# One chunk of the shared expert issued one tile earlier, the first tile's factors read from PSUM, and residual parts moved

## The chip, the core and the metric

The kernel runs on one core of a Trainium2 chip. The metric is the device time of one execution, in microseconds. Matrix products run on TensorE (PE), elementwise work on VectorE (DVE) and ScalarE (ACT), small powers and indirect DMAs on GpSimd (POOL), and SyncE (SP) issues the plain DMAs. The engines run beside each other and meet only at semaphores, each in the order in which its code is written.

## The reference

The input x has 2 batches of 1024 tokens with 512 values, all float32. From a 2 x 512 conditioning vector c come six modulation rows per batch. In short:

```
sa, ca, ga, sb, cb, gb = silu(c) @ wmod            # ga, gb: |.| at least 0.25, sign kept
h = layernorm(x) * (1 + ca) + sa
x = x + ga * attn(h)     # own layernorm, Q, K, V; A = sum over tokens of cos(K) * cos(V) after a rotary;
                         # Y = (0.5 * A + 0.5) * Q @ W_out + b_out + h
h = layernorm(x) * (1 + cb) + sb
x = x + gb * ffn(h)      # 8 experts with 2 per token, H = 352, and a shared one with HS = 704:
                         # silu(h @ w_gate) * (h @ w_up) @ w_down
```

## The kernel before

**Tiles.** The 2048 tokens are 16 tiles of 128 rows. Four tiles are one group `g` of 512 tokens. Nearly every product is split in high and low parts: an operand is written as `hi` (rounded) by ACT and as `lo` (the rest) by DVE, and `product3` (L1805 to L1807) issues hi*hi, hi*lo and lo*hi. So a matrix that TensorE is to read is ready when DVE has written its lo part, and the semaphore for it is counted by DVE.

**Start.** DVE computes the modulated and normalised row of tile 0: `modulated(0)` subtracts the mean and multiplies by `bc_c` (L1139), multiplies by 1/std and adds `bc_s` (L1142), and takes statistics of the row (L1143). `bc_c` is one plus a row that TensorE spread into PSUM, copied by DVE (L1252). POOL computes the power -0.5, ACT writes the normalised row (L735), TensorE transposes it (L1853), and ACT and DVE write hi and lo (`tokens_hi`, `tokens_lo`, L1150). The K and V products of tile 0 end with a bias product (L1871), whose row is finished by `bias_rows` on DVE (L1162).

**K and V for all 16 tiles**, and then a stage that builds the combined matrices `mw` (`m_block`, `m_first`, `m_second`). From here the residual of a tile is prepared by `residual_part(t)` (L1330) on DVE, which reads the row that ACT normalised in `x_normed(t)`.

**Second rows.** For each tile t, TensorE computes the attention output (`y_matmul(t)`: 12 products and a bias product, L2172). It waits for `x2_ready >= t - 1`, that is for `second_rows(t - 2)` on DVE, which empties the bank. DVE adds the residual (`second_rows`, L1342), takes statistics, then runs `residual_part(t + 1)`, `tokens2_lo(t - 2)` (L1361) and, when POOL has the power, `ffn_rows(t)` (L1354, L1356), the input of the expert part. TensorE transposes the ffn rows of tile t - 2 (`transposes2`, L2180), ACT writes their hi part and DVE their lo part. For t < 4 DVE also makes the lo part of a quarter of the shared weights (L1106). At tile 6, DVE multiplies and splits the four late blocks of `mw` for the second batch (L1294, L1299), which `y_matmul(8)` waits for.

Five chunks of the shared expert's gate and up products (24 products of 512 columns each, operands `xt` and `sgu`) of group 0 lie between these tiles or behind them. The table `Y_CHUNKS` says behind which tile a chunk stands: chunk 0 behind tile 6, then 7, 10, 13. Chunk 0 waits for `t2_lo >= 4`, the lo parts of tiles 0 to 3, and chunk 1 for `s_mul >= 1`, DVE's product of chunk 0 (L1369). ACT applies silu behind the chunk (`s_silu_of`); hi and lo parts of the result (`s_hi_of`, `s_lo_of`) follow one tile later.

**Shared and routed experts.** The shared expert goes on for groups 1 to 3, then the down products. Between the last ones TensorE transposes the 5 sub-tiles gathered for the first expert (`turn_rows`, L2092; the places are `TURN_AT`). Step s >= 2 waits for the lo part of step s - 2 (`picked_lo`, L1670). DVE also finishes output rows here (`shared_rows`, L1475 and L1477), two instructions for each tile. Then the routed experts run in a loop and at the end.

Of the kernel before, what the change touches and what calls it, by code (L numbers as in the profile page):

```python
# [21 lines left out]
ALU, ACT, AX = mybir.AluOpType, mybir.ActivationFunctionType, mybir.AxisListType  # L22
# [39 lines left out]

FIRST = 3
M_BLOCKS = 2 * DC - 1
Y_CHUNKS = {6: 0, 7: 1, 10: 2, 13: 3}


MISC = ["sin_a", "cos_a", "s1", "c1", "sin_b", "cos_b", "q0", "q1", "q2", "q3", "mod", "qrow", "qbias", "a0", "a1"]
# [5 lines left out]
def build(nc, X, W_in, b_in, W_out, b_out, gamma, beta, gate_w, w_gate, w_up, w_down,  # L74
# [10 lines left out]
    with ctx:  # L85
# [620 lines left out]
        def _(act):  # L706
# [192 lines left out]
            def s_hi_of(g, m):  # L899
                n = NS * g + m  # L900
                r = SM[m]
                act.wait_ge(s_mul, n + 1)
                if n == 0:
                    act.wait_ge(y_mm, NB)
                if g:
                    act.wait_ge(s_down_mm, GT * g)
                nc.scalar.activation(gtS[0:r, m, 0, :], gbuf_of(n)[0:r, :], ACT.Copy).then_inc(s_hi, 1)
# [22 lines left out]
            for t in range(NT):  # L930
                if t >= 6 and t % GT == 2:
                    read_parts((t - 6) // GT)
                if t >= 2:
                    tokens2_hi(t - 2)
                if t + 2 < NT:
                    x_normed(t + 2)
                if t in (FIRST + 1, FIRST + 2):
                    m_block_out(2 * (t - FIRST - 1))
                    m_block_out(2 * (t - FIRST - 1) + 1)
                if t == NB - 2:  # L940
                    for i in range(DC):
                        m_block_hi_late(i)
                if t - 1 in Y_CHUNKS:
                    s_hi_of(0, Y_CHUNKS[t - 1])
                if t in Y_CHUNKS:
                    s_silu_of(0, Y_CHUNKS[t])

# [146 lines left out]
        def _(dve):  # L1094
            steps = [0]

            def link(ins):

                steps[0] += 1
                ins.then_inc(dve_step, 1)  # L1100
                dve.wait_ge(dve_step, steps[0])
# [27 lines left out]
            def modulated(t):  # L1129

                b, row = t // NB, hz[:, t % 2, :]
                dve.wait_ge(rs1_ready, t + 1)
                if t >= 2:
                    dve.wait_ge(z_ready, t - 1)
                if t == 0:
                    dve.wait_ge(s0_ready, 1)
                if t == NB:
                    dve.wait_ge(misc_read, MISC.index("c1") + 1)
                dve.scalar_tensor_tensor(row, xring[:, t % GT, :], mv1[:, t, 0:1], bc_c[:, b, :], ALU.subtract, ALU.mult)\  # L1139
                    .then_inc(x_read, 1)  # L1140
                dve.wait_ge(x_read, t + 1)
                link(dve.scalar_tensor_tensor(row, row, rs[:, 0, t:t + 1], bc_s[:, b, :], ALU.mult, ALU.add))  # L1142
                link(dve.bn_stats(st6[:, :], row))  # L1143
                link(dve.bn_aggr(mv2[:, t, :], st6[:, :]))
                dve.tensor_scalar_add(ve[:, 1, t:t + 1], mv2[:, t, 1:2], EPS)
                dve.tensor_scalar_mul(mv2[:, t, 0:1], mv2[:, t, 0:1], -1.0).then_inc(ve2_ready, 1)

            def tokens_lo(t):
                dve.wait_ge(t_hi, t + 1)
                dve.tensor_tensor(tokens(t, 1), chunked(bank[T_BANKS[t % 2]][:, :]), tokens(t, 0).bitcast(F32),  # L1150
                                  ALU.subtract).then_inc(t_lo, 1)
# [96 lines left out]
            dve.tensor_copy(b_col[:, 2:4], bank[COL_BANK][:, at + 2 * DC:at + 2 * DC + 2]).then_inc(gb_ready, 1)  # L1248
            dve.wait_ge(gb_ready, 1)
            x_statistics(1)  # L1250
            dve.wait_ge(spread_mm, 3)
            link(dve.tensor_scalar_add(bc_c[:, 0, :], bank[V_BANKS[0]][:, :], 1.0))  # L1252
            modulated(0)
            weights_lo(0)
            x_statistics(2)
            tokens_lo(0)
            bias_rows(0)
            modulated(1)
            weights_lo(1)
            bias_rows(1)  # L1260
            tokens_lo(1)
# [127 lines left out]
            m_block(0, 1)  # L1389
            read_misc("a1")  # L1390
            m_block_lo(0, 1)
            m_block(0, 2)
            scaled_q_lo(1, 0)
            m_block_lo(0, 2)
            m_block(0, 3)
# [2 lines left out]
            scaled_q_lo(1, 1)  # L1398
            y_bias_rows()
            scaled_q_lo(1, 2)  # L1400
            residual_part(0)
            scaled_q_lo(1, 3)
            dve.wait_ge(cb_in, 16)
            dve.wait_ge(sb_in, 16)
            for t in range(NT):
                second_rows(t)
                if t + 1 < NT:
                    residual_part(t + 1)
                if t >= 2:
                    tokens2_lo(t - 2)  # L1410
                if t == NB - 2:
                    for i in range(DC):
                        m_block_late(i)
                if t - 1 in Y_CHUNKS:
                    s_lo_of(0, Y_CHUNKS[t - 1])
                ffn_rows(t)
                if t == NB - 2:
                    for i in range(DC):
                        m_block_lo_late(i)
                if t < DC:  # L1420
                    shared_in_lo(t)
                if t in Y_CHUNKS:
                    s_mul_of(0, Y_CHUNKS[t])
# [339 lines left out]
            expert_lo(0, 0, 2)  # L1763
            for s in range(CT):
                picked_lo(0, 0, (s,))
                if s < 2:
                    shared_rows(3, (s,))
            shared_rows(3, (2, 3))
            turn_columns(0, 0)
            dve.wait_ge(loops_ready, 1)  # L1770
# [512 lines left out]
```

## Time and profile before

| | |
|---|---|
| median of 3 runs | 666.33 us (665.25 to 667.1) |
| the profiled execution | 664.12 us, span 662.3 us |
| PE busy | 641.1 us, 97% |
| DVE busy | 494.9 us, 75% |
| ACT busy | 268.8 us, 41% |
| mean granted TensorE clock | 0.993 of full |

The span is what lies between the first and the last record, and 1.8 us of the execution lie around it. A busy PE means that a product was in flight. What matters for a change that moves instructions is where TensorE stood idle, for whom it waited, and when the clock that the chip granted was lower. In rows of the timeline the first number is the start and the second the time from start to end; products overlap, so the next one starts 0.23 us after the last although each takes 0.39 us.

### The profile page before, as it was taken

What the parts mean: (1) busy time and instruction counts of PE and PEld (TensorE: products, weight loads), DVE (VectorE), ACT (ScalarE), POOL (GpSimd) and SP (SyncE); (2) the same over time, 40 slices, a digit from 0 to 9 for tenths busy, and PEclk for the clock granted to TensorE, in tenths of its full rate; (3) what the DMA queues carried; (4) which work ended last, traced back from release to release, by engine and by line L of the source; (5) the groups of instructions that cost most, each with busy time, mean ns of one, the idle gap of its engine ahead of it and who ended that gap; (6) DMA issues with size and microseconds to landing.
All of it is one profiled execution on the core that took longest, in us unless ns stands there. A gap on an engine that the chain in (4) does not pass through costs nothing.

```text
span 662.3 us, 10575 instructions
## 1 busy us (share of the span) xinstructions
PE 641.1 (97%) x3666; PEld 531.5 (80%) x3666; DVE 494.9 (75%) x1086; ACT 268.8 (41%) x525; POOL 164.8 (25%) x211
## 2 busy tenths in 40 slices
PE   7899999999998999999999999999999999999995
PEld 3577677777876787888888788798989899899994
DVE  3987779847899788647886684659769697786953
ACT  3555354443453443412102301445537455474530
POOL 1233233320111111100000002223644455443123
PEclk9999999999998999999999999999999999999998
DMA  8923031006234262513042052446877667666144
GB/s 331 395 58 108 34 96 33 32 17 207 79 113 142 96 208 103 159 54 106 0 133 82 17 163 83 121 139 192 173 141 214 80 196 162 150 183 106 49 61 63
DMA packets 41151, 80.80 MB, mean 122 GB/s; under 512 B 5019, under 2 KB 13229, under 8 KB 40566
## 3 DMA queue, kind: packets, MB, share of 16 engines
q1 hardware_dynamic: 33382, 62.06, 28.6%
q0 software_dynamic: 7728, 18.22, 15.0%
q8 instruction: 23, 0.38, 0.2%
q14 instruction: 18, 0.15, 0.1%
HBM read 58.88 MB, written 22.56 MB: 123 GB/s over the span
## 4 chain that ended last, share of the span: by engine, by line
PE 83%; DVE 11%; issue 2%; ACT 1%; POOL 1%; DMA 1%; SPq 0%; POOLq 0%; DVEq 0%
PE bank L1805 22%; PE bank L1807 22%; PE bank L1806 22%; PE bank L2117 5%; PE bank L2092 2%; PE bank L1935 1%; PE bank L2122 1%; PE bank L1871 1%; PE bank L1853 1%; DMA xring<-in_L_attn_X 1%; PE bank L2072 1%; PE bank L2180 1%; DVE st L1121 1%; POOL out_rows L679 1%; DVE hx L1354 1%
## 5 line engine op out<-in xcount | busy, mean ns | idle before, releaser
L1805 PE MATMUL bank<-ht,ew 128*128 128x256 f32 (+1 forms) x256 | 74.3, 290 | 0.0
L1805 PE MATMUL bank<-xt,sgu 128*128 128x512 f32 x176 | 70.1, 398 | 3.6 <-DVE xt L1361 2.0
L679 POOL DMA_INDIRECT out_rows<-y,si x35 | 54.8, 1565 | 75.4 <-DVE y L1734 66.0
L1806 PE MATMUL bank<-ht,ew 128*128 128x256 f32 (+1 forms) x256 | 73.1, 285 | 0.0
L1807 PE MATMUL bank<-ht,ew 128*128 128x256 f32 (+1 forms) x256 | 73.0, 285 | 0.0
L1807 PE MATMUL bank<-xt,sgu 128*128 128x512 f32 x176 | 69.3, 394 | 0.0
L1806 PE MATMUL bank<-xt,sgu 128*128 128x512 f32 x176 | 69.2, 393 | 0.0
L1805 PE MATMUL bank<-wkv,xt 128*128 128x512 f32 x128 | 53.8, 421 | 0.7 <-DVE xt L1150 0.7
L1806 PE MATMUL bank<-wkv,xt 128*128 128x512 f32 x128 | 50.5, 394 | 0.0
L1807 PE MATMUL bank<-wkv,xt 128*128 128x512 f32 x128 | 50.4, 394 | 0.0
L1806 PEld LDWEIGHTS bank<-ht,ew 128*128 128x128 f32 x256 | 48.3, 188 | 0.0
L1805 PEld LDWEIGHTS bank<-ht,ew 128*128 128x128 f32 x256 | 48.2, 188 | 0.0
L1807 PEld LDWEIGHTS bank<-ht,ew 128*128 128x128 f32 x256 | 48.2, 188 | 0.0
L659 POOL COPY gi<-gidx 128x5 int32 (+1 forms) x8 | 4.7, 583 | 170.3 <-DVEq L1643 130.6
L667 POOL DMA_INDIRECT picked<-h_d,gi x36 | 41.3, 1146 | 17.5 <-issue 8.5
L1805 PEld LDWEIGHTS bank<-xt,sgu 128*128 128x128 f32 x176 | 33.4, 190 | 10.9 <-DVE xt L1361 2.2
L610 POOL TENSOR_TENSOR rs<-ve,nhalf 128x1 f32<-128x1 f32 x16 | 15.4, 961 | 96.5 <-DVE ve L1123 96.5
L1807 PEld LDWEIGHTS bank<-xt,sgu 128*128 128x128 f32 x176 | 33.4, 190 | 7.2
L1806 PEld LDWEIGHTS bank<-xt,sgu 128*128 128x128 f32 x176 | 33.5, 190 | 6.4
L1805 PE MATMUL bank<-ew,gtR 128*128 128x512 f32 (+1 forms) x96 | 38.4, 400 | 0.0
L1807 PE MATMUL bank<-ew,gtR 128*128 128x512 f32 (+1 forms) x96 | 37.9, 395 | 0.0
L1806 PE MATMUL bank<-ew,gtR 128*128 128x512 f32 (+1 forms) x96 | 37.9, 394 | 0.0
(374 smaller groups left out, 1631.5 us busy)
## 6 DMA issues: line engine op xcount, KB each, us to landing
xring<-in_L_attn_X SPq DMA_DIRECT2D x32, 256.0 KB, 2.7
ewst<-in_L_ffn_w_gate SPq DMA_DIRECT2D x8, 704.0 KB
ewst<-in_L_ffn_w_up SPq DMA_DIRECT2D x8, 704.0 KB
slots<-in_L_wmod SPq DMA_DIRECT2D x4, 1024.0 KB, 7.0
x_d<-rows SPq DMA_DIRECT2D x16, 256.0 KB, 2.0
h_d<-hx SPq DMA_DIRECT2D x16, 256.0 KB, 2.0
xrow<-x_d SPq DMA_DIRECT2D x16, 256.0 KB, 2.7
out_rows<-xrow SPq DMA_DIRECT2D x16, 256.0 KB, 2.0
```

The source lines that it names most:

```text
L610: pool.tensor_tensor(rs[:, 2, t:t + 1], ve[:, 2, t:t + 1], nhalf[:, 0:1], ALU.pow).then_inc(rs3_ready, 1)
L667: pool.indirect_dma_start(out=picked[par][:, j, :], out_offset=None, in_=h2_d, in_offset=bass.IndirectOffsetOnAxis(ap=gi[:, par, j:j + 1], ...
L679: pool.indirect_dma_start(out=out, out_offset=bass.IndirectOffsetOnAxis(ap=si[0:CR[j], par, j:j + 1], axis=0), in_=y[0:CR[j], j, :], in_of ...
L1121: link(dve.bn_stats(st6[:, :], row))
L1354: link(dve.scalar_tensor_tensor(hx_of(t), rows_of(t), mv2[:, t, 0:1], bc_cb[:, b, :], ALU.subtract, ALU.mult))
L1805: nc.tensor.matmul(dst, a[0], b[0], start=first, stop=False)
L1806: nc.tensor.matmul(dst, a[0], b[1], start=False, stop=False)
L1807: return nc.tensor.matmul(dst, a[1], b[0], start=False, stop=last)
L1853: last = nc.tensor.transpose(bank[T_BANKS[t % 2]][:, k * P:(k + 1) * P], hz[:, 2 + t % 2, k * P:(k + 1) * P], ident[:, :])
L1871: nc.tensor.matmul(to, pairs4[:, :].to_broadcast([P, P]), (bk, bv)[i][:, :], start=False, stop=True)\
L2092: last = nc.tensor.transpose(bank[RT_BANKS[(par + s) % 2]][:, i * P:(i + 1) * P], picked[par][:, j, k * P:(k + 1) * P], ident[:, :])
L2117: nc.tensor.matmul(bank[to[c % 2]][0:n, 0:width], packed[:, k, i * P:i * P + n], tok[part][:, k, :], start=k == 0 and not part, stop=k == ...
```

## The change

It has four parts, and none changes what is computed.

- Tile 0's row is made in another way. `modulated_first` computes (x - mean) / std first, multiplies by one plus the row in PSUM, and adds `bc_s`. The copy `bc_c` follows behind it. `modulated(1)` moves ahead of `bias_rows(0)`.
- `residual_part(0)` and `residual_part(1)` move from the end of the matrix stage, and from tile 0 of the second rows, into the matrix stage.
- Chunk 0 of the shared expert stands behind tile 5 in place of tile 6 on TensorE, ACT and DVE. `tokens2_lo(3)` stands ahead of `residual_part(6)` on DVE. The hi and lo parts of the chunk stay at tile 7, by the new table `Y_PARTS`.
- `shared_rows` of tiles 12 and 13 stand behind steps 1 and 2 of the first expert's lo parts, in place of steps 0 and 1.

```diff
-Y_CHUNKS = {6: 0, 7: 1, 10: 2, 13: 3}
+Y_CHUNKS = {5: 0, 7: 1, 10: 2, 13: 3}
+Y_PARTS = {7: 0, 8: 1, 11: 2, 14: 3}
...
-                if t - 1 in Y_CHUNKS:
-                    s_hi_of(0, Y_CHUNKS[t - 1])
+                if t in Y_PARTS:
+                    s_hi_of(0, Y_PARTS[t])
...
+            def modulated_first():
+
+                row = hz[:, 0, :]
+                dve.wait_ge(rs1_ready, 1)
+                dve.tensor_scalar(row, xring[:, 0, :], mv1[:, 0, 0:1], rs[:, 0, 0:1], ALU.subtract, ALU.mult).then_inc(x_read, 1)
+                dve.wait_ge(spread_mm, 3)
+                dve.wait_ge(x_read, 1)
+                link(dve.scalar_tensor_tensor(row, bank[V_BANKS[0]][:, :], 1.0, row, ALU.add, ALU.mult))
+                dve.wait_ge(s0_ready, 1)
+                link(dve.tensor_tensor(row, row, bc_s[:, 0, :], ALU.add))
+                statistics_of_h(0)
...
-            dve.wait_ge(spread_mm, 3)
+            modulated_first()
             link(dve.tensor_scalar_add(bc_c[:, 0, :], bank[V_BANKS[0]][:, :], 1.0))
-            modulated(0)
             weights_lo(0)
             x_statistics(2)
             tokens_lo(0)
+            modulated(1)
             bias_rows(0)
-            modulated(1)
             weights_lo(1)
...
             m_block_lo(0, 1)
+            residual_part(0)
             m_block(0, 2)
+            residual_part(1)
             scaled_q_lo(1, 0)
...
                 second_rows(t)
-                if t + 1 < NT:
+                if t == GT + 1:
+                    tokens2_lo(t - 2)
+                if t and t + 1 < NT:
                     residual_part(t + 1)
-                if t >= 2:
+                if t >= 2 and t != GT + 1:
                     tokens2_lo(t - 2)
...
                 picked_lo(0, 0, (s,))
-                if s < 2:
-                    shared_rows(3, (s,))
+                if s in (1, 2):
+                    shared_rows(3, (s - 1,))
```

On DVE at the start, `hz` is the row of tile 0 (then of tile 1), `bk` the bias row and `wkv` the lo parts of the K weights. Before:

```order
L1252 TENSOR_SCALAR bc_c<-bank 128x512
L1139 SCALAR_TENSOR_TENSOR hz<-xring,mv,bc_c 128x512
L1142 SCALAR_TENSOR_TENSOR hz<-hz,rs,bc_s 128x512
L1143 BN_STATS st<-hz 128x6
L1144 BN_AGGR mv<-st 128x2
L1145 TENSOR_SCALAR ve<-mv 128x1
L1146 TENSOR_SCALAR mv<-mv 128x1
L1156 SCALAR_TENSOR_TENSOR wkv<-slots,gb_col,wkv 128x512 x4
```

The same place now:

```order
L1148 TENSOR_SCALAR hz<-xring,mv,rs 128x512
L1151 SCALAR_TENSOR_TENSOR hz<-bank,hz 128x512
L1153 TENSOR_TENSOR hz<-hz,bc_s 128x512
L1158 BN_STATS st<-hz 128x6
L1159 BN_AGGR mv<-st 128x2
L1160 TENSOR_SCALAR ve<-mv 128x1
L1161 TENSOR_SCALAR mv<-mv 128x1
L1267 TENSOR_SCALAR bc_c<-bank 128x512
L1171 SCALAR_TENSOR_TENSOR wkv<-slots,gb_col,wkv 128x512 x4
```

The row has three instructions of its own, and the copy `bc_c` moved from ahead of it to behind it.

On TensorE, ahead of chunk 0 of the shared expert (`xt,sgu`); `bh,pair` ends an attention product, `tmp,gw` are the gate's logits of group 0, `ident,hx` transposes of ffn rows. Before:

```order
L2172 MATMUL bank<-bh,pair 128x512
L2193 MATMUL bank<-tmp,gw 32x128 x16
L2180 MATMUL bank<-ident,hx 128x128 x4
L1805 MATMUL bank<-xt,sgu 128x512
L1806 MATMUL bank<-xt,sgu 128x512
```

Now:

```order
L1824 MATMUL bank<-mw,xt 128x512
L2189 MATMUL bank<-bh,pair 128x512
L2197 MATMUL bank<-ident,hx 128x128 x4
L1822 MATMUL bank<-xt,sgu 128x512
L1823 MATMUL bank<-xt,sgu 128x512
```

These are the attention product of tile 5 and the transposes of tile 3. The product of tile 6, the logits and the transposes of tile 4 now come behind the chunk.

On DVE at tile 5 (`xt` is the lo part of tile 3, `u` the residual of tile 6, `ewst` the product of chunk 0). Before:

```order
L1342 SCALAR_TENSOR_TENSOR rows<-u,mv,bank 128x512
L1121 BN_STATS st<-rows 128x6
L1122 BN_AGGR mv<-st 128x2
L1123 TENSOR_SCALAR ve<-mv 128x1
L1330 SCALAR_TENSOR_TENSOR u<-bc_c,std,xring 128x512
L1361 TENSOR_TENSOR xt<-bank,xt 128x4x128
L1354 SCALAR_TENSOR_TENSOR hx<-rows,mv,bc_gb 128x512
L1356 SCALAR_TENSOR_TENSOR hx<-hx,rs,bc_s 128x512
```

Now:

```order
L1356 SCALAR_TENSOR_TENSOR rows<-u,mv,bank 128x512
L1122 BN_STATS st<-rows 128x6
L1123 BN_AGGR mv<-st 128x2
L1124 TENSOR_SCALAR ve<-mv 128x1
L1375 TENSOR_TENSOR xt<-bank,xt 128x4x128
L1344 SCALAR_TENSOR_TENSOR u<-bc_c,std,xring 128x512
L1368 SCALAR_TENSOR_TENSOR hx<-rows,mv,bc_gb 128x512
L1370 SCALAR_TENSOR_TENSOR hx<-hx,rs,bc_s 128x512
L1383 TENSOR_TENSOR ewst<-ewst,bank 128x512
```

The lo part moved one instruction ahead, and the product of chunk 0 came in from the end of tile 6.

## Rows read from the trace of the kernel before

**Rows 1.** The page: busy us, share of the span and instructions of each engine.

```profile
PE 641.1 (97%) x3666; PEld 531.5 (80%) x3666; DVE 494.9 (75%) x1086; ACT 268.8 (41%) x525; POOL 164.8 (25%) x211
```

**Rows 2.** Waits of TensorE: line, releaser, us in total, times, longest.

```profile
PE bank L1805 <- DVE rows L1342: 2.3, 2, 1.2
PE bank L1853 <- ACT hz L735: 2.1, 2, 1.8
PE bank L1805 <- DVE xt L1361: 2.0, 1, 2.0
```

**Rows 3.** Stretches: length, busy us of five engines (instructions), granted clock, DMA.

```profile
207.00:208.00 1.00, 1.00 (x4) 0.81 (x3) 0.93 (x4) 0.00 (x0) 0.00 (x0) 0.50 0.96 356
```

**Rows 4.** Timeline of TensorE: start, us, line, operation, tiles, shapes, idle before.

```profile
196.12 0.60 PE L2180 MATMUL bank<-ident,hx 128*128 128x128 f32 x4
197.91 0.50 PE L1805 MATMUL bank<-mw,xt 128*128 128x512 f32 x1 [1.19 <-DVE rows L1342]
...
202.15 0.65 PE L2180 MATMUL bank<-ident,hx 128*128 128x128 f32 x4
...
204.81 0.50 PE L1805 MATMUL bank<-xt,sgu 128*128 128x512 f32 x1 [2.00 <-DVE xt L1361]
...
212.00 0.40 PE L1805 MATMUL bank<-mw,xt 128*128 128x512 f32 x1
...
215.14 0.60 PE L2180 MATMUL bank<-ident,hx 128*128 128x128 f32 x4
216.17 0.50 PE L1805 MATMUL bank<-xt,sgu 128*128 128x512 f32 x1 [0.43 <-DVE ewst L1369]
...
221.75 0.40 PE L1805 MATMUL bank<-mw,xt 128*128 128x512 f32 x1
```

**Rows 5.** Timeline of VectorE, tiles 2 to 6 of the second rows.

```profile
187.49 0.69 DVE L1361 TENSOR_TENSOR xt<-bank,xt 128x512 fp32r<-128x512 f32 x1
...
203.41 0.74 DVE L1330 SCALAR_TENSOR_TENSOR u<-bc_c,std,xring 128x512 f32<-128x512 f32 x1
204.07 0.69 DVE L1361 TENSOR_TENSOR xt<-bank,xt 128x512 fp32r<-128x512 f32 x1
...
206.11 0.75 DVE L1342 SCALAR_TENSOR_TENSOR rows<-u,mv,bank 128x512 f32<-128x512 f32 x1
...
215.43 0.68 DVE L1369 TENSOR_TENSOR ewst<-ewst,bank 128x512 f32<-128x512 f32 x1
```

**Rows 6.** Timeline of ScalarE, hi part of tile 0's ffn rows.

```profile
186.86 0.60 ACT L880 ACTIVATE xt<-bank 128x512 fp32r<-128x512 f32 x1
```

**Rows 7.** Timeline of VectorE, the start.

```profile
14.22 0.75 DVE L1139 SCALAR_TENSOR_TENSOR hz<-xring,mv,bc_c 128x512 f32<-128x512 f32 x1 [0.91 <-ACT bc_s L806]
...
15.80 0.69 DVE L1143 BATCH_NORM_STATS2 st<-hz 128x6 f32<-128x512 f32 x1
...
20.55 0.69 DVE L1150 TENSOR_TENSOR xt<-bank,xt 128x512 fp32r<-128x512 f32 x1
21.16 0.74 DVE L1162 SCALAR_TENSOR_TENSOR bk<-bk,nodd,bank 128x512 fp32r<-128x512 f32 x1
21.81 0.75 DVE L1139 SCALAR_TENSOR_TENSOR hz<-xring,mv,bc_c 128x512 f32<-128x512 f32 x1
...
24.46 2.73 DVE L1156 SCALAR_TENSOR_TENSOR wkv<-slots,gb_col,wkv 128x512 fp32r<-128x512 f32 x4
```

**Rows 8.** Timeline of TensorE, tile 0's bias product and tile 1's transposes.

```profile
23.96 0.19 PEld L1871 LDWEIGHTS bank<-bk,pairs 128*128 128x128 f32 x1
...
26.81 0.66 PE L1853 MATMUL bank<-ident,hz 128*128 128x128 f32 x4 [0.26 <-ACT hz L735]
```

**Rows 9.** Timeline of ScalarE, VectorE and TensorE at the first expert's transposes.

```profile
424.50 0.60 ACT L985 ACTIVATE ht<-bank 128x512 fp32r<-128x512 f32 x1 [2.37 <-PE bank L2092]
...
426.29 0.68 DVE L1670 TENSOR_TENSOR ht<-bank,ht 128x512 fp32r<-128x512 f32 x1
...
427.03 0.66 PE L2092 MATMUL bank<-ident,picked 128*128 128x128 f32 x4 [1.21 <-DVE ht L1670]
```

More of the change, by code:

```diff
@@ L1134, in modulated @@
                     dve.wait_ge(z_ready, t - 1)
-                if t == 0:
-                    dve.wait_ge(s0_ready, 1)
                 if t == NB:
@@ L1142, in modulated, with statistics_of_h @@
                 link(dve.scalar_tensor_tensor(row, row, rs[:, 0, t:t + 1], bc_s[:, b, :], ALU.mult, ALU.add))
-                link(dve.bn_stats(st6[:, :], row))
+                statistics_of_h(t)
+            def modulated_first():
[8 more added lines that the diff above has]
+                statistics_of_h(0)
+            def statistics_of_h(t):
+                link(dve.bn_stats(st6[:, :], hz[:, t % 2, :]))
                 link(dve.bn_aggr(mv2[:, t, :], st6[:, :]))
@@ L1400, in _ @@
             scaled_q_lo(1, 2)
-            residual_part(0)
             scaled_q_lo(1, 3)
@@ L1413, in _ @@
                         m_block_late(i)
-                if t - 1 in Y_CHUNKS:
-                    s_lo_of(0, Y_CHUNKS[t - 1])
+                if t in Y_PARTS:
+                    s_lo_of(0, Y_PARTS[t])
                 ffn_rows(t)
```

## The prediction

> **What bounds the kernel now.** The page comes first. TensorE is busy for 641.1 of 662.3 us [rows 1], so time is won or lost only where it stands idle or runs slowly. The waits of TensorE say where: 2.3 us in two waits for DVE's second rows, 2.1 us for ACT's normalised rows at the start, 2.0 us once for the lo part of a tile [rows 2]. The timeline of TensorE then places them. Around tiles 5 to 7 there are three waits, of 1.19, 2.00 and 0.43 us [rows 4], and the stretches show that the granted clock fell to half, 1.2 GHz, shortly after the second of them, and was there at 207 to 208 us [rows 3]. The reader is to see that chunk 0 of the shared expert took 204.81 to 212.00, 7.19 us, and chunk 1, the same 24 products at 2.4 GHz, 216.17 to 221.75, 5.58 us [rows 4]: the low clock cost 1.6 us. What bounds this stretch is DVE. It runs from tile 2 on without a stop worth naming, and it makes the lo parts that TensorE waits for [rows 5]. At the end of the shared expert TensorE waits 1.21 us more for DVE [rows 9]. So three places count, and I take them one by one.
>
> **The chunk behind tile 5.** TensorE has done the transposes of tile 3 at about 196.5 (they start at 196.12 [rows 4]). Now the product of tile 6 came next, and it waited 1.19 us. In the changed kernel the chunk comes next, and it needs the lo part of tile 3. DVE wrote that from 204.07 to 204.76 [rows 5]. Put ahead of the residual part, which runs from 203.41 to 204.07, it starts at 203.41 and ends at 204.10, 0.66 us earlier. TensorE starts the chunk 0.05 us behind, at 204.15, and not at 204.81. So of the 7.6 us from 196.5 to 204.15 it does nothing, where before 4.7 us of useful work, tile 6's product, logits and transposes, stood among them.
>
> Could DVE be earlier? The two residual parts that leave this chain are worth 0.66 us each. The one of tile 1 lay beside POOL's power at tile 0, so its going saves nothing. The one of tile 0 lets DVE run 0.66 us ahead, but only up to the lo part of tile 0. That starts at 187.49, right behind ACT's hi part (186.86 + 0.60 = 187.46 [rows 5, 6]), which waits for TensorE's transposes. TensorE works there without a wait, so this point doesn't move and DVE waits off what it had won. In the matrix stage the two residual parts fall into idle time of DVE ahead of `m_block(0, 2)` and of `scaled_q_lo(1, 0)`, where it waits for TensorE and ACT: nothing. Had that cover not been there, they would cost at most 2 x 0.66 on DVE, and TensorE has work to do meanwhile.
>
> From 204.15 on the pieces have the lengths that the timeline shows [rows 4]. The chunk takes 5.58. Tile 6's product, logits and transposes took 197.91 to the end of the transposes, 202.15 + 0.65 = 202.80, less 0.24 because the next product may start that much ahead of a modelled end: 4.65, and 0.1 less again since the product doesn't start from a stop. Tile 7's product with logits and transposes takes from 212.00 to 215.14 + 0.60 less 0.24: 3.5. Chunk 1 takes 5.58. The sum is 223.4 for the start of tile 8's product, which stood at 221.75 [rows 4]: later by 1.6 us, with no low clock in it, where the 221.75 has 1.6 us of it. The small wait of 0.43 for chunk 0's product is gone, for DVE now makes that product while TensorE runs tile 6.
>
> What is late next? DVE can't take tile 6's rows before TensorE has made its product, at 204.15 + 5.58 + about 3.2 = 212.9 in place of 206.11. From there to the end of the four late lo parts of `mw` it took 206.11 to 215.43, 9.3 us [rows 5], and some 0.2 more as the lo part of tile 4 now waits for its transposes. So 222.5, against 223.4 when TensorE asks for them. 0.9 us is left. DVE then has about 3 us of arrears on tiles 7 and 8, which TensorE doesn't feel: it asks for tile 7's rows at tile 9.
>
> **The clock.** Before, waits of 1.19 and 2.00 us close together were followed by the low clock, 1.2 GHz [rows 3, 4]. The changed kernel has one wait of over 7 us in that place. The nearest row is that fall, with its cost of 1.6 us, and I take it again. The ends are 0 (no fall, or one that has passed within the wait) and 5.6 us (the whole chunk at half speed costs its 5.58 us once more). So the stretch costs 1.6 + 1.6 = 3.2 us, between 1.6 and 7.2.
>
> The Trainium skill (TensorE: Matmul & The Clock Gate, the section on why this matters for your kernel) says that a long gap between bursts of matmuls brings the clock back to the lower level and that only sustained work raises it again. The trace agrees for a wait of 2.00 us. By this rule, too, it is worse to gather several short waits into one long one, and the fall would be sure: the 3.2 us stand. Without the rule the sum would be the same, with more weight on its lower end.
>
> **The start.** The three instructions of tile 0's row: the first is done while the copy `bc_c` ran, the second ends about when ACT's `bc_s` comes (14.22 is when DVE went on behind it [rows 7]), and the third, an add of 0.69 us as others of 512 columns [rows 7], puts the statistics at 14.94 in place of 15.80: 0.86 us earlier. But behind them comes the copy, which I size like the add, 0.69 and 0.03 for its hand-over, ahead of the lo parts of the weights. So `tokens_lo(0)` starts at 20.55 - 0.86 + 0.72 = 20.41, and TensorE's K products only 0.14 us earlier. The first instruction, a form that no row of the trace shows with 512 columns out of SBUF, may take anything up to the 0.75 of its neighbours without mattering.
>
> Then `modulated(1)` stands ahead of `bias_rows(0)`. It starts at 20.41 + 0.61 = 21.02 and takes 2.65 (21.81 to 24.46), so the bias row starts at 23.67 and is there at 24.41 (0.74). TensorE wanted it at 23.96, now 23.82 [rows 7, 8]: a new wait of 0.6, after which it is 0.45 behind. Tile 1's transposes follow, which had waited 0.26 for their row [rows 8]; the row is earlier now, so 0.45 - 0.26 = 0.2 us is left. Queued behind the late bias row on DVE are the lo parts of the V weights, which start as before. I take +0.2. The ends are -0.9 (all that the row gained) and +0.5.
>
> **The first expert's transposes.** ACT has the hi part of step 1 at 424.50 + 0.60 = 425.10. DVE was in the output rows of tile 12 and took the lo part at 426.29; TensorE waited for it until 427.03 [rows 9]. Moved ahead, the lo part runs from 425.13 to 425.81 and TensorE goes on at 425.87: -1.15 us. The output rows, 1.3 us for each tile, come 0.7 and 1.3 us later, ahead of steps 2 and 3, whose lo parts TensorE wants only after 15 further products, some 3.5 us on. The ends are -1.2 and -0.5.
>
> **The sum**, on the profiled execution: 664.12 + 3.2 + 0.2 - 1.15 = 666.4 us. The median of the runs, 666.33, is 2.2 above the profiled execution. On it the same +2.3 gives 668.6 us. What a measurement can tell from no change is about 0.3%, 2.0 us, so slower begins at 668.3 and faster ends at 664.3.
>
> **Rivals.**
>
> *The clock costs nothing more.* Over the long wait the clock falls and is up again when the chunk starts, or soon after. For it: behind the wait of 1.19 alone the products kept their usual pace (197.91 to 202.15 for tile 6 and the logits [rows 4]). Against it: behind the one of 2.00 us they did not. Then 1.6 + 0.2 - 1.15 = +0.65: 667.0, within 0.3%. This is the case on the other side, not slower. It decides from the point where the low clock costs under 1.3 us.
>
> *DVE keeps its lead.* If the lo part of tile 0 isn't held up by ACT, the chunk starts 0.66 us earlier, at 203.5: 668.0. Against it: the two rows meet within 0.03 us [rows 5, 6].
>
> *DVE's arrears reach TensorE.* The late lo parts of `mw` have 0.9 us to spare. If a wait that I don't see takes 2 us on DVE at tile 6, tile 8's product waits 1.1: 669.7.
>
> *The low clock lasts.* The whole chunk runs at half speed: 5.6 in place of 1.6, 672.6.
>
> *The chunk finds its tile ready.* If what chunk 0 waited for were there by 197, the three waits and the low clock would go, 3.6 + 1.6, and with the expert's 1.15 and the start's 0.2 the time would be 666.33 - 6.2 = 660.2. Against it stands the DVE row at 204.07, which is in order behind five tiles.
>
> **How the numbers follow.** Forecast 0.55; no cost of the clock 0.15; DVE's lead 0.05; arrears 0.11; long low clock 0.09; tile ready 0.05. The forecast lies close to the 2.0 us. I give it 0.37 beyond and 0.18 within: the wait over 7 us stands in every run, while the low clock of before is seen in one execution, and a median without it would raise the difference. Slower is 0.37 + 0.11 + 0.09 = 0.57, same 0.18 + 0.15 + 0.05 = 0.38, faster 0.05. The range goes from 666.4 (the clock for nothing, and the start winning half of its 0.9) to 670.2 (the forecast with the low clock twice as long).
>
> **What would show it.** The wait of TensorE for DVE's `xt` line should stand at 6.5 to 7.5 us in one piece ahead of the chunk, the waits for `rows` at tile 6 and for `ewst` at chunk 1 gone, the clock at half behind it, and the wait for `ht` under 0.2. Near 24 us there should be a wait of about 0.6 for the `bk` row. Tile 8's product should start 3 to 3.5 us later than at 221.75. I am wrong if the long wait is under 4 us, or if the chunk runs at full clock.

## The result, and the profile after

The changed kernel takes 666.7 us, the median of 20 executions (665.59 to 668.46). The kernel before, executed again beside it, takes 665.38 us in 20 executions (663.85 to 667.1). The ratio is 1.0021, with an interval from 1.0013 to 1.0028: slower by 1.3 us, and inside the 0.3% that the forecast had called no change. The forecast was 668.6 us and "slower by over 0.3%" at 0.57, so its likeliest case did not come. Two sets of executions below hold one of a slow state each (1287.64 us in before_fill1, 2621.3 us of the kernel before beside it), which moves their medians by under 0.03 us.

The profiled execution of the changed kernel took 666.73 us, with a span of 664.9 us, against 664.12 and 662.3 before. Between the two profiled executions stand +2.6 us, where the working had +2.3. What the change does in the stage and at the expert came nearly as worked out; what went wrong lies between one execution and the median.

The page of the changed kernel begins as follows (busy us, share of the span, instructions; then the granted clock in tenths, in 40 slices).

```profile
PE 642.0 (97%) x3666; PEld 532.7 (80%) x3666; DVE 495.1 (74%) x1087; ACT 268.3 (40%) x525; POOL 162.4 (24%) x211
PEclk9899999999997999999999999999999999999999
```

TensorE is as busy as in [rows 1]. Two slices stand out, an 8 at the start and a 7 in the slice from about 199 to 216 us. The waits of TensorE in the changed kernel (line, releaser, us in total, times, longest) are these:

```profile
PE bank L1822 <- DVE xt L1375: 7.4, 1, 7.4
PE bank L1822 <- DVE xt L1165: 1.4, 1, 1.4
PE bank L1822 <- DVE rows L1356: 1.1, 1, 1.1
PE bank L1870 <- ACT hz L736: 1.0, 1, 1.0
```

The 2.0 us for `xt` and one of the two waits for `rows` of [rows 2] have become one wait of 7.4 us, and the waits for `ewst` and `ht` are off the list. The timeline of TensorE (start, us, line, operation, tiles, idle before) shows the long wait and what follows:

```profile
197.09 0.60 PE L2197 MATMUL bank<-ident,hx 128*128 128x128 f32 x4
...
205.10 0.80 PE L1822 MATMUL bank<-xt,sgu 128*128 128x512 f32 x1 [7.42 <-DVE xt L1375]
...
212.26 0.40 PE L1822 MATMUL bank<-mw,xt 128*128 128x512 f32 x1
...
220.36 0.47 PE L1822 MATMUL bank<-xt,sgu 128*128 128x512 f32 x1
...
225.93 0.40 PE L1822 MATMUL bank<-mw,xt 128*128 128x512 f32 x1
```

Chunk 0 took 205.10 to 212.26, 7.16 us, its first product 0.80 us long. Tile 8's product starts at 225.93, 4.2 us later than in [rows 4]. Of these, 0.97 us come from the start, since the first transposes of the second rows stand at 186.70 and stood at 185.73; the stage itself is 3.2 us longer. The granted clock (the number behind the five engines' busy times) accounts for the long chunk:

```profile
21.00:22.00 1.00, 0.84 (x2) 0.75 (x3) 0.96 (x3) 1.00 (x2) 0.00 (x0) 0.50 1.10 414
...
200.00:202.00 2.00, 0.00 (x0) 0.00 (x0) 1.97 (x4) 0.66 (x2) 0.99 (x1) 0.92 0.72 202
202.00:204.00 2.00, 0.00 (x0) 0.00 (x0) 1.97 (x3) 0.00 (x0) 0.00 (x0) 0.50 0.25 92
204.00:206.00 2.00, 0.90 (x2) 0.80 (x3) 1.93 (x6) 0.00 (x0) 0.55 (x1) 0.50 0.82 301
...
208.00:209.00 1.00, 1.00 (x5) 0.83 (x4) 0.00 (x0) 0.00 (x0) 0.00 (x0) 0.75 0.70 260
```

The clock fell to 1.2 GHz inside the long wait, at about 201.7 us, and came back at about 208.5, so the first 3.4 us of the chunk ran at half. There is a second low stretch, at 21 us, which the profile of before does not have. VectorE's timeline in the stage:

```profile
204.36 0.68 DVE L1375 TENSOR_TENSOR xt<-bank,xt 128x512 fp32r<-128x512 f32 x1
204.96 0.74 DVE L1344 SCALAR_TENSOR_TENSOR u<-bc_c,std,xring 128x512 f32<-128x512 f32 x1
...
213.09 0.69 DVE L1383 TENSOR_TENSOR ewst<-ewst,bank 128x512 f32<-128x512 f32 x1 [5.93 <-ACT ewst L898]
...
215.49 0.75 DVE L1356 SCALAR_TENSOR_TENSOR rows<-u,mv,bank 128x512 f32<-128x512 f32 x1 [1.71 <-PE bank L2189]
```

The lo part stands ahead of the residual part, as written. DVE, which had no stop worth naming here before, is idle for 5.93 and 1.71 us: the idle time of TensorE has been answered by idle time of DVE behind it.

At the start (VectorE, then TensorE):

```profile
12.65 0.54 DVE L1148 TENSOR_SCALAR hz<-xring,mv,rs 128x512 f32<-128x512 f32 x1
...
14.96 0.69 DVE L1158 BATCH_NORM_STATS2 st<-hz 128x6 f32<-128x512 f32 x1
...
16.04 0.68 DVE L1267 TENSOR_SCALAR bc_c<-bank 128x512 f32<-128x512 f32 x1
...
20.42 0.68 DVE L1165 TENSOR_TENSOR xt<-bank,xt 128x512 fp32r<-128x512 f32 x1
...
23.66 0.74 DVE L1177 SCALAR_TENSOR_TENSOR bk<-bk,nodd,bank 128x512 fp32r<-128x512 f32 x1
```

```profile
18.46 0.66 PE L1870 MATMUL bank<-ident,hz 128*128 128x128 f32 x4 [1.01 <-ACT hz L736]
21.16 0.80 PE L1822 MATMUL bank<-wkv,xt 128*128 128x512 f32 x1 [1.37 <-DVE xt L1165]
...
25.43 0.39 PE L1888 MATMUL bank<-bk,pairs 128*128 128x512 f32 x1
...
27.72 0.66 PE L1870 MATMUL bank<-ident,hz 128*128 128x128 f32 x4
```

The statistics start at 14.96, tile 0's transposes 0.77 us earlier, and the K products 0.14 us earlier. Their wait is thereby 1.37 us and no longer 0.74. These products ran at 1.2 GHz, 4.27 us for twelve (21.16 to 25.43) where they had taken 2.90, so tile 1's transposes are 0.91 us late [rows 8]. At the first expert:

```profile
428.63 0.60 ACT L986 ACTIVATE ht<-bank 128x512 fp32r<-128x512 f32 x1 [2.37 <-PE bank L2109]
...
429.26 0.69 DVE L1687 TENSOR_TENSOR ht<-bank,ht 128x512 fp32r<-128x512 f32 x1 [2.27 <-ACT ht L986]
...
430.01 0.66 PE L2109 MATMUL bank<-ident,picked 128*128 128x128 f32 x4
```

From the first transposes of this expert's turn to the fourth it is 5.88 us (424.13 to 430.01) and was 7.03 (420.00 to 427.03 [rows 9]): 1.15 us less.

### The profile page after: what moved, and what is told of

Its sections match the earlier page's. It is cut to its first block, busy times and chain, and to the rows that moved or that the text cites. A ratio compares the mean times of both kernels' runs of the same rounds, so it can differ in the third digit from the quotient of the medians.

```text
span 664.9 us, 10578 instructions
## 1 busy us (share of the span) xinstructions
PE 642.0 (97%) x3666; PEld 532.7 (80%) x3666; DVE 495.1 (74%) x1087; ACT 268.3 (40%) x525; POOL 162.4 (24%) x211
## 4 chain that ended last, share of the span: by engine, by line
PE 86%; DVE 9%; issue 1%; ACT 1%; DMA 1%; POOL 1%; SPq 0%; POOLq 0%; DVEq 0%
PE bank L1822 23%; PE bank L1823 22%; PE bank L1824 22%; PE bank L2134 5%; PE bank L2109 2%; PE bank L1952 1%; PE bank L2139 1%; PE bank L1888 1%; PE bank L2197 1%; PE bank L1870 1%; DMA xring<-in_L_attn_X 1%; PE bank L2089 1%; POOL out_rows L680 1%; PE bank L2210 1%; PE bank L1851 1%
## 5 line engine op out<-in xcount | busy, mean ns | idle before, releaser
L1822 PE MATMUL bank<-wkv,xt 128*128 128x512 f32 x128 | 54.5, 426 | 1.4 <-DVE xt L1165 1.4
L1823 PE MATMUL bank<-wkv,xt 128*128 128x512 f32 x128 | 51.0, 398 | 0.0
L1824 PE MATMUL bank<-wkv,xt 128*128 128x512 f32 x128 | 50.9, 398 | 0.0
L660 POOL COPY gi<-gidx 128x5 int32 (+1 forms) x8 | 3.0, 378 | 169.0 <-DVEq L1660 130.5
```

Of the source, the lines that this page charges most:

```text
L1822: nc.tensor.matmul(dst, a[0], b[0], start=first, stop=False)
L1823: nc.tensor.matmul(dst, a[0], b[1], start=False, stop=False)
L1824: return nc.tensor.matmul(dst, a[1], b[0], start=False, stop=last)
```

## The experiments

Three theories were weighed. The first: the low clock behind the long wait makes the change slower. The rival: it is the waits alone, the clock costs nothing more. The third came with the result: the profiled execution of before was a lucky one, and the kernel before has low stretches of its own that its profile doesn't show. A "fall" below is a stretch at 1.2 GHz.

### The kernel before once more, and the parts alone

The first group holds the kernel before unchanged, the part for the chunk alone, the part for the experts alone, and the changed kernel with the chunk put back.

```diff
 before_again: nothing
 chunk_only, on the kernel before:
-Y_CHUNKS = {6: 0, 7: 1, 10: 2, 13: 3}
+Y_CHUNKS = {5: 0, 7: 1, 10: 2, 13: 3}
+Y_PARTS = {7: 0, 8: 1, 11: 2, 14: 3}
+                if t == GT + 1:
+                    tokens2_lo(t - 2)
 experts_only, on the kernel before:
-                if s < 2:
-                    shared_rows(3, (s,))
+                if s in (1, 2):
+                    shared_rows(3, (s - 1,))
 no_chunk, on the changed kernel:
+Y_CHUNKS = {6: 0, 7: 1, 10: 2, 13: 3}
```

> The kernel before once more, unchanged. The forecast's sum of +2.3 us was made against one profiled execution of it (664.12 us), and between the two profiled executions the change did cost +2.6 us, while the medians differ by only 1.3 us. Theory A: that profiled execution is on the fast side by 1.3 us, since how often and where the TensorE clock falls differs between executions of the same kernel, and the median execution of before already pays for one more fall, at the start or near tile 6. Then the median comes out at 665.0 to 665.8, ratio 1.000 within 0.001, and the mean granted clocks of its executions scatter between 0.988 and 0.994, the slow ones at the low end. Theory B: the clock is the same in all executions of before (0.993 in all, scatter without pattern), and the missing 1.3 us is a term of the sum that was taken too large.

> Only the move of chunk 0 behind tile 5, with tile 3's lo part ahead of the residual part; start, residual parts and output rows as before. By the sum +3.2 us against the profiled execution of before (ratio 1.005). Theory A: less than that in the medians, +1.5 to +2.4 us, ratio 1.0025 to 1.0035, because the median of before holds a clock fall that its profile doesn't show, while this kernel's one long wait always brings one. Theory B (the term itself is too large): under +1.5 us and the wait ahead of the chunk under 6 us in its profile.

> Only the output rows of tiles 12 and 13 one step later, so that the lo part of step 1 comes first. By the sum -1.15 us, ratio 0.9983, in both theories. The wait of TensorE for the ht line at 427 us is gone. If the ratio is under 0.997, the missing 1.3 us were won here.

> The changed kernel with chunk 0 back behind tile 6, all else as changed, tile 3's lo part ahead too. By the sum: start +0.2, experts -1.15, and the wait ahead of the chunk shorter by 0.66: -1.6 us, ratio 0.9976. If the start pays a clock fall in the typical execution, as the changed kernel's profile shows (0.8 us), -0.8 us, ratio 0.9988. Against the changed kernel that is -2.1 to -2.9 us. A chunk term that is too large (theory B) would make this kernel no faster than -1 us against the changed one.

Measured, against 665.6 us of the kernel before on that chip (26 executions; the ratio is on record with its interval and isn't the quotient of the two medians, from which it differs by up to 0.0012):

| kernel | median us (executions) | ratio, interval |
|---|---|---|
| before_again | 665.66 (12) | 0.999, 0.9978 to 1.0001 |
| chunk_only | 669.1 (7) | 1.0041, 1.0025 to 1.0056 |
| experts_only | 664.24 (12) | 0.9976, 0.9966 to 0.9986 |
| no_chunk | 664.51 (8) | 0.9979, 0.9962 to 0.9995 |

Of the expectations, those for before_again (theory A), experts_only and no_chunk came within 0.5 us; the mean clocks of before_again scatter between 0.991 and 0.997, where 0.988 to 0.994 had been expected. The one for chunk_only did not: theory A gave it +1.5 to +2.4 us and theory B less, and it costs 3.5 us against 665.6, by its ratio 1.7 to 3.7.

The same program, profiled again in before_again, took 666.99 us, 2.9 us more than its first profile. Its stretches show why:

```profile
22.00:24.00 2.00, 1.94 (x5) 1.55 (x6) 1.97 (x4) 1.60 (x3) 0.00 (x0) 0.50 1.03 387
24.00:26.00 2.00, 2.00 (x6) 1.59 (x5) 1.90 (x7) 0.00 (x0) 0.61 (x1) 0.50 1.12 423
26.00:28.00 2.00, 2.00 (x9) 1.09 (x11) 1.95 (x3) 0.82 (x1) 1.62 (x3) 0.50 0.96 376
...
209.00:210.00 1.00, 1.00 (x4) 0.76 (x4) 1.00 (x2) 0.00 (x0) 0.00 (x0) 0.53 0.00 0
```

A fall of nearly 7 us at the start, which the first profile does not have, put tile 1's transposes at 29.97 in place of 26.81 (0.8 us of this stood before the fall). The fall in chunk 0 is there too, 1.5 us behind the chunk's start, as it was 1.4 us behind in the first profile.

In experts_only chunk 0 ran at 2.4 GHz throughout, and the next wait is the telling one (TensorE's timeline, then two stretches):

```profile
204.68 0.50 PE L1805 MATMUL bank<-xt,sgu 128*128 128x512 f32 x1 [1.99 <-DVE xt L1361]
...
216.03 0.50 PE L1805 MATMUL bank<-xt,sgu 128*128 128x512 f32 x1 [2.01 <-DVE ewst L1369]
```

```profile
217.00:218.00 1.00, 1.00 (x4) 0.82 (x4) 0.93 (x4) 0.00 (x0) 0.15 (x1) 0.63 0.50 190
218.00:219.00 1.00, 1.00 (x4) 0.71 (x4) 1.00 (x3) 0.00 (x0) 0.83 (x1) 0.50 0.21 72
```

Where chunk 0 is fast, TensorE waits 2.01 us for DVE's product `ewst`, and with the fall it waited 0.43 [rows 4]. Chunk 1 starts equally far behind the first transposes of the stage, 30.42 us here (185.61 to 216.03) and 30.44 before (185.73 to 216.17). So the fall in chunk 0, which I had counted at 1.6 us, cost the kernel before nothing: DVE sets the start of chunk 1. Here it was chunk 1 that had the fall, with nothing behind it to hide it, and tile 8's product came 1.6 us later.

The parts: chunk_only alone costs 3.4 us against before_again (669.1 and 665.66) and experts_only wins 1.4. In no_chunk, tile 3's lo part ahead of the residual part only changes which wait it is: 1.34 us for `xt` and 2.70 for `ewst`, with chunk 1 again 30.42 us behind the first transposes. The moved residual parts show nowhere. chunk_only has them in their old places, and its long wait is the same:

```profile
205.43 0.79 PE L1808 MATMUL bank<-xt,sgu 128*128 128x512 f32 x1 [7.41 <-DVE xt L1362]
```

Its profiled execution (669.15 us) had a low stretch of 3.4 us at the start, just behind the first K product, and tile 1's transposes at 28.04 in place of 26.81. From the first transposes of the second rows to tile 8's product it took 39.49 us, 3.5 more than the first profile of before.

### Waits without falls: before_warm and after_warm

To take the falls away and leave the waits, I put idle products (128x128, their result unused) into TensorE's waits, at the start and at tiles 5 to 7.

```diff
-            keep_busy(8)
+            keep_busy(13)            (after_warm: 11)
...
-            keep_busy(3)
+            keep_busy(5)             (after_warm: 7)
+FILL = {6: 6, 7: 6}                  (after_warm: {5: 20})
+                if t in FILL:
+                    pe.wait_ge(x2_ready, t)
+                    keep_busy(FILL[t], Y_BANKS[(t + 1) % 2])
```

> The kernel before with idle products put where TensorE waits: 13 in place of 8 and 5 in place of 3 at the start, and 6 each ahead of chunks 0 and 1, into banks that are free. They end before the waits do. Theory A (the median of before pays for clock falls that its first profile doesn't show): the falls go, the executions of this kernel lie closer together, and the median falls by 1.0 to 2.0 us (ratio 0.997 to 0.9985), mean clock 0.996 or more in nearly all. Theory B (the scatter has nothing to do with the clock): ratio 1.000 and the same spread of 2.8 us.

> The changed kernel with idle products at the same places: 11 in place of 8 and 7 in place of 3 at the start, and 20 in the long wait ahead of chunk 0. Theory A: the fall ahead of chunk 0 (1.4 to 1.6 us, in every execution) and the one at the start (0.8 us, in most) go: 2.0 to 2.6 us below the changed kernel, that is 664.1 to 664.7. Against before_warm the difference is then the waits alone: 1.6 + 0.2 - 1.15 = +0.6 us. Theory B: no more than 0.5 us faster than the changed kernel.

before_warm measured 663.88 us (12 executions, 663.37 to 664.91) against 665.25 of before on that chip: 0.9982, 0.9973 to 0.9992. after_warm measured 664.27 (11, 663.97 to 665.18): 0.9992, 0.9983 to 1.0002. In both profiles the granted clock is 1.00 from 20 to 25 and from 196 to 224 us. In the rows below, a group of 20 idle products counts as 40 records. TensorE's waits at the chunks, before_warm:

```profile
204.74 0.50 PE L1806 MATMUL bank<-xt,sgu 128*128 128x512 f32 x1 [0.67 <-DVE xt L1362]
216.10 0.50 PE L1806 MATMUL bank<-xt,sgu 128*128 128x512 f32 x1 [0.70 <-DVE ewst L1370]
```

and after_warm:

```profile
197.74 4.73 PE L1833 MATMUL bank<-ident 128*128 128x128 f32 x40 [1.19 <-DVE rows L1357]
203.97 0.50 PE L1823 MATMUL bank<-xt,sgu 128*128 128x512 f32 x1 [1.50 <-DVE xt L1376]
```

The idle products fill most of each wait, and the real ones start no later. Two things follow. Without falls the change is worth +0.39 us (664.27 - 663.88; by the two ratios it is 0.7). By the pieces of the two profiles: the stage to chunk 1 is 32.08 against 30.43 us, +1.65; the expert's turn 5.88 against 7.03, -1.15; the start -0.1; together +0.4. And the falls cost the kernel before about 1.4 us in the median (665.25 - 663.88), the changed kernel 2.4 (666.70 - 664.27, from two sets, beside which the medians of before were 665.38 and 665.25). The 2.4 is also what the two falls in its profile cost by their pieces: 39.23 us from the first transposes to tile 8's product against 37.65 in after_warm, 1.58, and at the start 6.56 us from the first K product to tile 1's transposes against 5.69, 0.87. The same pieces show the hidden fall: this stage takes 36.02 us in the first profile of before, with a fall in chunk 0, and 36.03 in before_warm, with none. So both theories have a share: of the 1.3 us, some 0.4 are waits with the start and the expert, and 1.0 is the clock, net.

### The start alone, and an order that keeps DVE's product out of the way

```diff
 start_only, on the kernel before: modulated_first() in place of modulated(0),
-            bias_rows(0)
             modulated(1)
+            bias_rows(0)
 mul_first, on experts_only: the lo part of tile 3 ahead of the residual part, and
                 ffn_rows(t)
+                if t in Y_CHUNKS:
+                    s_mul_of(0, Y_CHUNKS[t])
                 ...
                 m_block_lo_late(i)
-                if t in Y_CHUNKS:
-                    s_mul_of(0, Y_CHUNKS[t])
```

> Only the new start: tile 0's row from the bank, modulated(1) ahead of bias_rows(0). The forecast's term is +0.2 us (ratio 1.0003). If the order of modulated(1) and bias_rows(0) lets the clock fall more often or longer than before, +0.5 to +1.0. The sum of the parts as measured so far (chunk +2.7 to +3.5, output rows -1.4, all +1.4) leaves -0.7 to +0.1 for the start and the residual parts: if the new start wins, the ratio is 0.999.

> A version that should beat both: the kernel before with the output rows moved, tile 3's lo part ahead, chunk 0 left behind tile 6, and DVE's product of chunk 0 ahead of the four late lo parts of mw at tile 6. In the kernel before chunk 1 starts when DVE has that product, 30.4 us behind the first transposes of the second rows whatever the clock does in chunk 0. It should start at 213.8 in place of 216.2: -2.4 us, and -1.15 from the output rows, together -3.6 us, ratio 0.9946. If the late lo parts then hold up tile 8's product, 1 us less. With the wait ahead of chunk 1 gone, no fall of the clock in chunk 1 either.

start_only measured 663.87 us (12 executions, 663.25 to 666.09), ratio 0.9984, 0.9975 to 0.9994. Its profiled execution was one of its slowest, 666.09, with low stretches at 20.5 to 24 and in chunk 1, and tile 1's transposes at 27.54. So its profile doesn't show the gain of its median. The gain of 1.4 us was in none of the expectations (+0.2, +0.5 to +1.0, or a ratio of 0.999). Three of its twelve executions took over 664.5 us, and 24 of the 29 of the kernel before beside it.

mul_first measured 660.28 us (5 executions, 660.06 to 660.91), ratio 0.993, 0.9917 to 0.9944: it beats both kernels. TensorE's timeline:

```profile
204.50 0.50 PE L1807 MATMUL bank<-xt,sgu 128*128 128x512 f32 x1 [1.34 <-DVE xt L1361]
214.11 0.50 PE L1807 MATMUL bank<-xt,sgu 128*128 128x512 f32 x1 [0.29 <-DVE ewst L1369]
```

and VectorE's:

```profile
213.38 0.68 DVE L1369 TENSOR_TENSOR ewst<-ewst,bank 128x512 f32<-128x512 f32 x1
213.97 1.28 DVE L1299 TENSOR_TENSOR mw<-xrow,mw 128x512 fp32r<-128x512 f32 x2
```

The product stood at 215.43 behind the four lo parts of `mw` [rows 5] and now stands ahead of them, at 213.38. Chunk 1 starts 28.03 us behind the stage's first transposes, 2.4 us earlier; with the expert's 1.15 that is 3.55 us, and 663.88 of before_warm less 660.28 is 3.6. The profile shows no fall at the start or in the chunks, and the five executions lie within 0.9 us, so the falls seem to have gone too, which makes the difference to the kernel before about 5 us. The order of the lo part of tile 3 alone left chunk 1 where it was (no_chunk, 30.42 us); the product's place brought it forward.

### One place of falls at a time, and the best of all

```diff
 before_fill1:     FILL = {7: 6}, the start as before
 before_fillstart: keep_busy(13) and keep_busy(5), no FILL
 after_fill0:      FILL = {5: 20}, the start as in the changed kernel
 best3:            mul_first with the new start and keep_busy(11), keep_busy(7)
```

> The kernel before with six idle products ahead of chunk 1 alone, where TensorE waits 2.0 us for DVE's product of chunk 0 in every execution in which chunk 0 ran at full clock. Theory A1: the fall that the median execution of before pays for lies here, in chunk 1, at 1.6 us each; then the median falls by 0.9 to 1.6 us (ratio 0.9976 to 0.9987), close to before_warm. Theory A2: it lies at the start; then the ratio is 1.000 within 0.0007.

> The kernel before with more idle products at the start alone (13 in place of 8, 5 in place of 3). Theory A1: the ratio is 1.000 within 0.0007. Theory A2: 0.9976 to 0.9987. If both places take part, each of the two kernels wins about half of the 1.4 us that before_warm won.

> The changed kernel with the 20 idle products ahead of chunk 0 alone. The fall that follows the long wait goes, which stands in every execution: 1.4 to 1.6 us below the changed kernel, 665.0 to 665.3, ratio to before 0.999 to 1.000. The start's fall stays (0.8 us above after_warm). A rival, that the long wait's fall costs nothing: no difference to the changed kernel, 666.5 to 666.9.

> mul_first with the new start and with more idle products there (11 in place of 8, 7 in place of 3). By the milestones of after_warm the new start alone is worth 0.1 us without falls, and mul_first's executions without a fall stand at 660.1. If the new start helps only by its falls, as its -1.4 us in the medians suggests, the fill makes it equal and this is 660.0 within 0.4 us. If it is worth 1 us of its own, 659.2.

| kernel | median us (executions) | ratio to before (665.01), interval |
|---|---|---|
| before_fill1 | 664.6 (12) | 0.9992, 0.9982 to 1.0001 |
| before_fillstart | 663.99 (12) | 0.9994, 0.9983 to 1.0005 |
| after_fill0 | 664.37 (12) | 0.9995, 0.9985 to 1.0004 |
| best3 | 660.43 (6) | 0.9931, 0.9919 to 0.9944 |

Eleven executions of before_fill1 fall into two groups: five executions at 663.56 to 663.9 with a mean clock of 0.996 to 0.997, and six at 664.6 to 665.4 with 0.992 to 0.995, of which the profiled one has its low stretch at 21.3 to 24.7 us. before_fillstart has eight at 663.4 to 664.6 and four at 665.0 to 665.8, and here the mean clock does not part them: 0.993 to 0.997 and 0.995 to 0.996. A fall in chunk 0 lowers the mean and costs nothing, as in the profiled execution (663.81 us, low from 205.6 to 209.0). The mean is blurred further by a low stretch that stands at the end of every profile, 2.1 to 6.1 us long. By the pieces of the profiles, a fall of 3.4 us costs 0.8 to 1.2 us at the start and 1.6 in chunk 1. The intervals of both ratios reach 1, so which of the two places counts more isn't shown. The medians point at the start: filling it alone brought them down by 1.0 us, and filling ahead of chunk 1 alone by 0.4, though the two ratios don't part them. So does chunk_only: it has no wait ahead of chunk 1 in its profile, but a fall at the start, and costs 3.5 us. In after_fill0 the start was left free to have its falls, yet its profile has no fall there, and it is as fast as after_warm; 665.0 to 665.3 had been expected. mul_first, with the start of before, had none there either in its profile. Why the start was spared in these is open. best3 gains nothing over mul_first.

## Why the prediction was wrong

**Where it held.** The chunk's long wait was to be 6.5 to 7.5 us in one piece; it was 7.42. The low clock was to follow it, and to cost 1.6; chunk 0 took 7.16 in place of 5.58. The waits were to cost 1.6 beside that; after_warm against before_warm has +1.65. The late lo parts of `mw` did not reach TensorE, and tile 8's product came 3.2 us later by the stage's own measure. The forecast's 3.5 at most was passed, 4.2, because the start added 0.97. The expert's -1.15 is -1.15. The lo part started at 204.36 and not 203.41, by 0.95 us, which is the late start again. The clock rule of the Trainium skill (TensorE: Matmul & The Clock Gate, Why this matters for your kernels), that a long gap brings the lower level, holds here in both profiled executions with the 7.4 us wait. For the wait of 2.00 us the prediction's "the trace agrees" said too much: the Trainium skill's rule there is about longer gaps, and behind waits of 2.0 us ahead of chunk 0 the fall came in some profiles (before, before_again, before_fillstart) and not in others (experts_only, start_only, before_fill1).

**Where it failed.** The step is the last of the sum: "The median of the runs, 666.33, is 2.2 above the profiled execution. On it the same +2.3 gives 668.6". It took the profiled execution and the median for the same kernel with an offset. They differ by falls. Of 83 executions of the kernel before that were run beside the experiments, 16 took up to 664.4 us and 5 over 666.6; most lie between. The one profiled, 664.12, belongs to the fastest fifth: its one fall lay in chunk 0, where DVE's product `ewst` hides it. I read this fall as 1.6 us of cost: "the 221.75 has 1.6 us of it". It has none, since with chunk 0 at full speed the wait for `ewst` is 2.0 us, and tile 8's product starts as far behind the first transposes (36.00 us in before_fill1, 36.03 in before_warm, 36.02 with the fall). The median execution of before pays about 1.4 us for a fall elsewhere, at the start or in chunk 1 behind that wait of 2.0. So the clock term between medians is 2.4 - 1.4 = +1.0, where I had +1.6, and the waits with the start and the expert are +0.4, where I had +0.65. That these make up the measured 1.3 is no check of its own, since all are differences of the same medians. The changed kernel has no wait ahead of chunk 1 in its profile, so it may be spared the fall there; but chunk_only has none there either and costs 3.5 us, so this alone doesn't bring the difference down.

The other part of the error is the base. 666.33 was the median of three executions; twenty give 665.38. Of the 1.9 us between 668.6 and 666.7 this is 0.95, and the difference itself 0.95 (2.3 against 1.3). The text had the first in view ("the low clock of before is seen in one execution, and a median without it would raise the difference") and drew the wrong conclusion: it had asked whether other executions lack the fall that was seen, not whether they have others.

**The start**, +0.2. Free of falls it is -0.1 (the first transposes of the second rows at 185.56 in after_warm and 185.67 in before_warm). The wait of 0.6 for `bk` did not show: at 1.2 GHz the products ahead asked for it only at 25.43, when it had been there since 24.40, and in after_warm that wait is 0.2. What I left out is that the earlier transposes make one longer wait, 1.37 for 0.74, and in the profile of the changed kernel a fall follows it, worth 0.9 us. But start_only has the same wait, and its median is 1.4 us under that of before. Its profiled execution took 666.09 us, 2.2 over its median, and says nothing on those at the median. Set against its term of the sum, the start is the part that missed most on the median: -1.4 for +0.2, where the chunk is +3.5 for +3.2 and the expert -1.4 for -1.15. The three add up to +0.7 and not to 1.3, so parts measured alone don't simply add. Whether the new start makes falls there rarer isn't settled: that only three of twelve in start_only took over 664.5 us speaks for it, but in the changed kernel 15 of 20 executions took 666.38 us or more, where the fall behind the long wait alone would give some 665.9 (an estimate, 664.27 + 1.58).

**The rivals.** "The clock costs nothing more" was given 667.0, and the time came out within 0.3 us of it, but the mechanism is not that one: the clock did cost the chunk 1.6. It came out there because the kernel before pays for falls too. The other rivals did not occur. Not tried was the kernel before with its chunk 0 forced to fall in each execution, which would show the hidden case at the median. *DVE keeps its lead* is answered by chunk_only, whose wait is 7.41 us without the moved residual parts and 7.42 with them.

## What to carry to other kernels

A profile is one execution. When its time is off the median by as much as the effect that is forecast, ask first which stretches of low clock it has or lacks, and profile the kernel before a second time, before its numbers are put onto the median. A low clock costs only what the engine that waits at the end of the stage lets through: look for the wait that shrank beside it. And where one engine sets the pace of a stage, an instruction of it that the other waits for goes ahead of those that nobody waits for yet; here the chunk's product, moved ahead of four lo parts, with one lo part moved ahead of a residual part, brought the next chunk 2.4 us forward.

## What the runs showed of the hardware

- Waits of 2.0 us and less were followed by a fall to 1.2 GHz in some profiles and not in others, with the same code up to that place: behind 2.00 us in [rows 3, 4], but not behind 1.99 in experts_only, where it came behind the next, of 2.01. The Trainium skill (TensorE: Matmul & The Clock Gate, Part 1) says of the rise to the higher level that its point varies from run to run; what these traces show to vary is whether and where the clock falls.
- At the start, a fall came with waits of 1.0 and 1.4 us (the changed kernel) and of 1.8 and 0.7 us (before_again), and began inside the second of them. The low stretch was 3.4 us long in the one and 6.8 in the other, where the way from the first K product to tile 1's transposes took 2.4 us more than in the first profile (22.06 to 29.97 against 21.30 to 26.81).
- With idle products of 128x128 in the waits, the profiles of before_warm and after_warm have no fall until the last 4 us, and no real product is later. The other executions lie close to them (663.37 to 664.91 and 663.97 to 665.18 us); their means of 0.996 to 0.998 don't exclude a fall that costs nothing, since experts_only and before_fillstart have 0.996 with one.
- In every profile the clock was low over the last 2.1 to 6.1 us of the span, so the mean granted clock of an execution doesn't tell how many falls stood before that.
- A DVE TENSOR_SCALAR of 128x512 with a source in SBUF took 0.54 us; the one out of a bank took 0.68.
